# Attention with FFN beside it: query scratch stored once and split on load, head stores ahead of loads, first head's rows loaded earlier

## What is computed

```python
xn = _layernorm(x)
q = _rope(split(xn @ Wq + bq)); k = _rope(split(xn @ Wk + bk)); v = split(xn @ Wv + bv)
scores = jnp.einsum('bhnd,bhmd->bhnm', q, k) / jnp.sqrt(256)
inter = jnp.einsum('bhnm,bhmd->bhnd', softmax(scores), v)
attn = inter @ Wo + bo
# FFN with weights +1/-1 from booleans; h starts as [xn, -xn]
h = relu(s0 * (h @ w0)) * 2; h = relu(s1 * (h @ w1)) * 2; h = s2 * (h @ w2)
return x + attn + h
```

## Time and profile before

| | |
|---|---|
| median of 3 runs (lowest, highest) | 2648.79 us (2647.93, 2649.21) |
| profiled execution, its own time | 2645.93 us |
| its span, first to last instruction | 2644.1 us |
| busy: TensorE, ScalarE, VectorE, GpSimd | 2577.4, 2099.3, 977.5, 300.0 us |
| preparation (to 240.48 us), attention (from there) | 240.48, 2403.62 us |

### The profile page before, as it was taken

The page is one execution under the profiler, slowest core; times in us unless marked ns, Lnnn a source line. Parts: engine busy times, 40 slices in busy tenths (PEclk is TensorE's granted clock), DMA queues, the critical chain, the costliest instruction groups (busy, mean ns, idle before and its releaser), DMA issues.

```text
span 2644.1 us, 49178 instructions
## 1 busy us (share of the span) xinstructions
PE 2577.4 (97%) x20711; PEld 1340.4 (51%) x20711; DVE 977.5 (37%) x1665; ACT 2099.3 (79%) x2342; POOL 300.0 (11%) x268
## 2 busy tenths in 40 slices
PE   7886999999999999999999999999999999999999
PEld 5663454444445454545445454544445454544545
DVE  7773323343324233243324233243324233242323
ACT  6885888888888878788887878788887878788884
POOL 6783000000000000000000000000000000000000
PEclk9997999999999999999999999999999999999999
DMA  9995111111212112121212212121212212121212
GB/s 283 294 292 171 37 47 52 53 61 49 57 43 75 51 48 71 50 77 53 78 44 70 63 46 70 53 77 51 77 43 67 61 53 69 57 77 49 77 38 97
DMA packets 202199, 210.45 MB, mean 80 GB/s; under 512 B 144685, under 2 KB 148605, under 8 KB 195577
## 3 DMA queue, kind: packets, MB, share of 16 engines
q1 hardware_dynamic: 199672, 198.91, 25.1%
q10 hardware_dynamic: 2304, 8.39, 0.9%
HBM read 131.34 MB, written 75.89 MB: 78 GB/s over the span
## 4 chain that ended last, share of the span: by engine, by line
PE 91%; ACT 0%; DVE 0%; issue 0%; DVEq 0%; SPq 0%
PE ps_o L1042 37%; PE ps_f L1075 27%; PE ps_s L1029 24%; PE ps_y L1088 2%; PE ps_s L1124 0%; PE ps_f L1124 0%; ACT probs L1009 0%; DVE probs L1266 0%; PE ps_f L1132 0%; PE ps_o L1124 0%; PE ps_y L1124 0%; PE ps_s L1132 0%; DVEq L819 0%; PE ps_o L1132 0%; PE ps_y L1132 0%
## 5 line engine op out<-in xcount | busy, mean ns | idle before, releaser
L1009 ACT ACTIVATE probs<-ps_s 128x1024 f32<-128x1024 f32 x2048 | 1930.0, 1034 | 453.1 <-PE ps_s L1029 450.7
L1042 PE MATMUL ps_o<-probs,v_ones 128*32 128x512 f32 x8192 | 1011.3, 600 | 0.0
L1029 PE MATMUL ps_s<-q_rows,k_rows 50*128 50x512 f32 x4096 | 868.9, 439 | 5.1 <-SPq L981 4.1
L1029 PEld LDWEIGHTS ps_s<-q_rows,k_rows 50*128 50x128 f32 x4096 | 365.7, 184 | 672.2 <-ACT probs L1009 600.3
L1042 PEld LDWEIGHTS ps_o<-probs,v_ones 128*32 128x32 f32 x8192 | 200.6, 108 | 418.3 <-issue 295.8
L1075 PE MATMUL ps_f<-h_hi,ffn_w 64*128 64x512 f32 x2048 | 410.2, 393 | 0.0
L1075 PE MATMUL ps_f<-h_lo,ffn_w 64*128 64x512 f32 x2048 | 409.3, 391 | 0.0
L1209 DVE COPY raw<-ps_f 128x512 f32<-128x512 f32 x256 | 164.9, 686 | 560.4 <-PE ps_f L1075 560.4
L1164 POOL TENSOR_TENSOR heads<-heads,sums 128x512 f32<-128x512 f32 x64 | 82.3, 1285 | 2149.8 <-DVE sums L1185 2149.8
L1185 DVE RECIPROCAL sums<-sums 128x128 f32<-128x128 f32 x256 | 226.6, 924 | 1.7
L1075 PEld LDWEIGHTS ps_f<-h_lo,ffn_w 64*128 64x128 f32 x2048 | 198.7, 186 | 34.2
(11 more groups left out here) (118 smaller groups left out, 1384.6 us busy)
## 6 DMA issues: line engine op xcount, KB each, us to landing
k_rows<-k_parts SPq DMA_DIRECT2D x128, 256.0 KB
q_rows<-q_parts SPq DMA_DIRECT2D x384, 64.0 KB
q_parts<-parts SPq DMA_DIRECT2D x32, 512.0 KB, 8.7
k_parts<-parts SPq DMA_DIRECT2D x32, 512.0 KB, 8.3
k_rows<-k_parts SPq DMA_DIRECT2D x128, 128.0 KB
x_chunk<-in_x ACTq DMA_DIRECT2D x16, 512.0 KB, 7.3
xn_d<-xn_t SPq DMA_DIRECT2D x16, 512.0 KB, 8.6
v_heads<-v_sb SPq DMA_DIRECT2D x16, 512.0 KB, 7.7
```

What stands on the lines that cost most here:

```text
L1009: nc.scalar.activation(probs[:, s % PBUF, half * 2 * C:(half + 1) * 2 * C], ps_s[:, half].rearrange("p c n -> p (c n)"), ACT.Exp, scale=SC ...
L1029: last = nc.tensor.matmul(ps_s[:, half, w], k_rows[rows, u, t * P:(t + 1) * P], q_rows[rows, u, half], start=True, stop=True)
L1042: last = nc.tensor.matmul(ps_o[32 * c:32 * c + 2 * DH], v_ones[:, u, t], probs[:, s % PBUF, c * C:(c + 1) * C], start=(t == 0), stop=(t == ...
```

## The change

**Queries.** The scratch for q holds the full fp32 value once (2 tiles per chunk of 128x512) instead of a high and a low part. GpSimd writes q's `turned` tile straight into `parts` (two buffers per j, by `c % 2`), ScalarE only squares it, SP stores it. For k nothing changes but the indices. On load, the three row groups of a head all read the same q rows. VectorE then rounds the whole tile into `q_hi` and subtracts `q_hi` times a mask that is 1 on the low rows only: the low rows become the low part, the others keep the full value, which the matmul reads as fp32r. This runs in the seventh round (n % 10 == 6) of the head before. The loads of a head are split into queries, shift and keys, in that order, with a semaphore of their own for queries and shift.

**First head.** Its queries are loaded at chunk 7, xT_lo at 8, its keys at 9 and 11 (halves). GpSimd splits the queries at the end of chunk 8 (three operations). The rows' zeroing moves from DMAs to a GpSimd memset. `store_shift` of the bound moves from SP's to ScalarE's queue. `bv` and `bo` are loaded at chunk 4 instead of 5. One small table `lo_rows` (128x1) is loaded ahead of Wv.

**Heads.** `heads` and `sums` have one buffer instead of two. `store_head` is ahead of `load_head`. `finish` waits for all earlier heads' stores and for GpSimd's product of the last head.

```diff
-FIRST_HEAD_AT = 13
+FIRST_QUERIES_AT = 7
+SPLIT_QUERIES_AT = 6
...
+                if c == FIRST_QUERIES_AT:
+                    sp.wait_ge(k_rows_set, 1)
+                    load_queries(sp, scratch, 0, w["q_rows"][:, 0], first_q_loaded)
+                if c == FIRST_QUERIES_AT + 1:
+                    sp.dma_start(w["xT_lo"][:].bitcast(F32).rearrange("p k n -> p (k n)"), scratch["xn"][0]).then_inc(first_x_loaded, 16)
+                if c in (FIRST_QUERIES_AT + 2, FIRST_QUERIES_AT + 4):
+                    load_keys(sp, scratch, 0, w["k_rows"][:, 0], first_loaded, [(c - FIRST_QUERIES_AT) // 2 - 1])
...
             def part(n):
-                c, j, u = n // 4, n % 4, n % PART_BUFS
+                c, j = n // 4, n % 4
...
-                nc.scalar.activation(square[:, c % 2, j], turned[:, n % 3], ACT.Square).then_inc(square_ready, 1)
-                if n >= PART_BUFS:
-                    act.wait_ge(parts_stored[u], 16 * (n // PART_BUFS))
-                nc.scalar.activation(parts[:, u, 0], turned[:, n % 3], ACT.Copy).then_inc(part_high, 1)
+                if j < 2:
+                    nc.scalar.activation(square[:, c % 2, j], parts[:, j, c % 2].bitcast(F32), ACT.Square).then_inc(square_ready, 1)
+                    return
+                k_out_of = turned[:, (2 * c + j - 2) % 3]
+                nc.scalar.activation(square[:, c % 2, j], k_out_of, ACT.Square).then_inc(square_ready, 1)
+                if c > 0:
+                    act.wait_ge(parts_stored[j], 16 * c)
+                nc.scalar.activation(parts[:, j, 0], k_out_of, ACT.Copy).then_inc(part_high, 1)
...
+                if c == FIRST_QUERIES_AT + 1:
+                    pool.wait_ge(first_q_loaded, 16 * 6)
+                    nc.gpsimd.tensor_copy(w["q_hi"][:].bitcast(F32R), first_q.bitcast(F32)).then_inc(first_q_high, 1)
...
+                    nc.gpsimd.tensor_tensor(w["q_hi"][:], w["q_hi"][:], w["lo_rows"][:, 0:1].broadcast_to([P, 2 * C]), ALU.mult).then_inc(first_q_high, 1)
...
+                    nc.gpsimd.tensor_tensor(first_q, first_q.bitcast(F32), w["q_hi"][:], ALU.subtract)
...
             def load_head(g, u):
-                load_rows(sp, scratch, g, q_rows[:, u], k_rows[:, u], rows_loaded[u])
+                load_queries(sp, scratch, g, q_rows[:, u], q_loaded[u])
+                load_shift(sp, scratch, g, q_rows[:, u], q_loaded[u])
+                load_keys(sp, scratch, g, k_rows[:, u], rows_loaded[u])
...
+                    if HEADS * i + j > 0:
+                        pe.wait_ge(q_split, HEADS * i + j)
...
             def finish(i, j):
-                u = j % 2
-                dve.wait_ge(heads_stored[u], 32 * CB * i + 16 * CB * (j // 2 + 1))
+                for u in range(2):
+                    dve.wait_ge(heads_stored[u], 16 * CB * ((HEADS * i + j + 1 - u) // 2 + 1))
+                    dve.sem_inc(tail_begun, 1)
+                if HEADS * i + j > 0:
+                    dve.wait_ge(heads_ready, HEADS * i + j)
+                    dve.sem_inc(tail_begun, 1)
...
+            def split_queries(g):
+                u = g % 2
+                at = q_rows[:, u].rearrange("p h n -> p (h n)")
+                dve.wait_ge(q_loaded[u], 16 * QUERY_LOADS * ((g + 1) // 2))
+                nc.vector.tensor_copy(q_hi[:].bitcast(F32R), at.bitcast(F32)).then_inc(q_step, 1)
+                dve.wait_ge(q_step, g)
+                dve.sem_inc(tail_begun, 1)
+                nc.vector.scalar_tensor_tensor(out=at, in0=q_hi[:], scalar=w["minus_lo"][:, 0:1], in1=at.bitcast(F32),
+                                               op0=ALU.mult, op1=ALU.add).then_inc(q_split, 1)
```

More of the change, by code:

```diff
@@ L266, in prepare, with store_shift @@
         block = ctx.enter_context(nc.Block())
+        def store_shift(queue, a, filled, landed):
+            to = scratch["shift"][a].rearrange("g (h w n) -> w (g h) n", h=P // G, n=FILL)
+            for n in range(G * N // (P * FILL)):
+                queue.dma_start(to[n], filled.bitcast(F32)).then_inc(landed, 16)
         def here(c):
@@ L272, in _ @@
         def _(sp):
-            def store_shift(a, filled, landed):
-                to = scratch["shift"][a].rearrange("g (h w n) -> w (g h) n", h=P // G, n=FILL)
-                for n in range(G * N // (P * FILL)):
-                    sp.dma_start(to[n], filled.bitcast(F32)).then_inc(landed, 16)
             sp.dma_start(ident[:], a["ident"]).then_inc(ident_loaded, 16)
@@ L292, in _ @@
             sp.wait_ge(zero_ready, 1)
[L293 removed]
+            store_shift(sp, 1, fill[:], fill_stored)
             def store_x(c):
@@ L851, in attend @@
         rows_loaded = [sem(f"rows_loaded{u}") for u in range(2)]
+        q_loaded = [sem(f"q_loaded{u}") for u in range(2)]
         v_loaded = [sem(f"v_loaded{u}") for u in range(2)]
@@ L953, in one_pass @@
                     u = j % 2
+                    if j == HEADS - 1 and last:
+                        begin_last()
+                    if j >= 1:
+                        store_head(i, j - 1)
                     if not last or j < 2:
```

187 lines of the change are left out of this document (110 added, 77 removed).

## The result

The changed kernel takes 2623.72 us (median; 2623.01 to 2623.82, four runs), the kernel before on the same chip 2648.36 us (2647.56 to 2649.21, four runs). The ratio is 0.9906, 95% interval 0.9889 to 0.9923: 24.6 us or 0.9% faster. The profiled execution took 2623.64 us with a span of 2621.9 us, against 2645.93 and 2644.1 before.

The account below looks back on a forecast made before the run. It took TensorE to bound attention, and bytes, closely followed by ScalarE and TensorE, the preparation's chunks. -13.4 - 2.5 - 11 + 6 + 3 = -17.9 from 2645.93 gave 2628.0, plus 2.86 for the median: 2631 us, range 2614 to 2643.

Parts of the forecast that it names:

- Ten chunks: Preparation from 63.83 us: smaller query stores and two fewer ScalarE copies bring chunks from 12.64 to 11.3 us, 13.4 us gained.
- The moved loads: First head's loads, now in chunks 7 to 11, delay key stores: about 2 us for each of three batches, 6 us lost.
- GpSimd's split: First head's queries: three GpSimd operations, at most 8.0 us, with 3.3 us free per chunk; 3 us lost.
- Last three chunks: End of the preparation, without the loads at chunks 13 and 14: 27.9 us instead of 38.93, 11 us gained, ends 8 to 15.
- Chunks 0 to 2: Start of the preparation: 1.6 MB fewer bytes, 5 us, of which half was taken: 2.5 us gained.
- Tail: Serial stretch between last chunks and attention: `store_shift` on ScalarE's queue changes 0, ends -1.9 and +1.
- attention: Attention stage: VectorE's added split, 121 us of work in 63 heads, fits into slack; 0, ends 0 and +3.
- B: Rival, 12%: bytes decide throughout and the moved loads fit into slack; 8.4 MB less at 291 GB/s is 28.8 us, 2620.
- A: Rival, 20%: ScalarE's work, not the bytes, bounds the chunks; 16.6 us gained less 9 for moved work, about 2641.
- C: Rival, 8%: the first head's work at chunks 7 to 11 eats the gain; no gain, about 2648.
- D: Rival, 5%: in attention the split comes too late for TensorE; slower, from 2660 to 2752.
- what was to show the steps right: Signs: ten chunks in about 113 us, last three in 28, no ScalarE query-store waits, key-store wait, GpSimd block 5 to 8, attention undisturbed.

Follow-up runs that it names:

- e_factors: The changed kernel with VectorE's `factors` of a chunk moved behind the fourth pair of products: 2618.0 us, ratio 0.9887.
- e_spread: The changed kernel with GpSimd's three operations on the first head's queries spread over the ends of chunks 8, 9 and 10: 2620.96 us, ratio 0.9901.
- e_before_early: The kernel before with only the first head's loads moved, from chunks 13 and 14 to 7 and 8: 2646.18 us, ratio 0.9995.
- e_bytes: The changed kernel with each query store issued twice, the second to a scratch that nothing reads (8.4 MB back): 2642.64 us, ratio 0.9982.
- e_split3: The changed kernel with VectorE's rounding of a head's queries to their high part made three times instead of once, in 63 heads: 2622.29 us, ratio 0.9907.
- e_shift_sp: The changed kernel with the first head's row of bounds stored by SyncE, as in the kernel before, instead of ScalarE: 2623.93 us, ratio 0.9912.
- e_act: The changed kernel with two ScalarE copies per chunk added in place of those removed, result unused: 2630.64 us, ratio 0.9937.

## Why the prediction came out as it did

The forecast was 2631.0 us in a range of 2614 to 2643; measured were 2623.72 and a gain of 24.6 where the sum had 17.9. Step by step:

- **Ten chunks, pace 11.3 us (-13.4).** The size was right, the reason was not: that is luck. Ten chunks of 11.37 us would be 113.7, 12.7 less than before; the stalls (1.7 and 0.5 at the loads, 3.9 for GpSimd's block with the short chunk behind it) make up the rest of the 119.77. But I took 11.3 as a mixture of bytes (10.8), ScalarE (10.5) and TensorE (10.1), three busy sums. What sets it is a circle through three engines with no single one full: VectorE is busy for 101.94 of 119.77 us, ScalarE for 97.66, GpSimd for 81.72. Cutting it (e_factors) gave chunks of 10 to 11 us. Before, ScalarE's work did fill such a chunk, and I subtracted two copies from it without following what the chunk would wait for next. Half of that could be read before: VectorE waited for ScalarE there, and `shift_ln` took up to 0.96 us in other chunks.
- **The moved loads (+6).** Three stalls of 2 us were expected. The first measured 1.7 us (13.04 - 11.37), the last 0.5 (11.88), and the one between them is hidden in GpSimd's block; in e_spread, where it isn't, the three make 4.4 us. So three stalls came as expected, somewhat smaller: the term was too dear by 4 us as the kernel stands and by 1.6 without the block. The working behind it is not sound. The 7.2 us were those of a half and of xT_lo, 1088 KB, and I scaled them as if they were the half's 576 alone; 384 of 1088 KB give 2.5 us, which the 3 us of slack would have covered. And the slack is larger, for a key store lands in 4.8 us now (median) and not in the 8.3 that I left standing: 6.5 us instead of 3. That stalls are left all the same shows that landing behind such a batch takes more than either sum had: the store that ScalarE waits for until 116.91 was issued from 107.14 on. By the rule of the Trainium skill that I weighed ("DMA: Bandwidth & Descriptors", section on why a DMA increments its semaphore by 16), these stalls would have been nearer 12 us; the waits are against it. No row shows single DMA engines, so only its price falls here, not the rule.
- **GpSimd's split (+3).** Its chunk grew by 5.2 us, its full 5.3, and the next one gave 1.3 back: 3.9 us, near the forecast. The 3.3 us of free time were not free where the block stands, for GpSimd stands in the circle. e_spread got 2.3 us of the pair back (1.6 over the ten chunks), and what stays there is the stall of the key loads.
- **Last three chunks (-11).** They gave 16.27, the largest error. I priced them as 11.2 + 11.2 + 5.5; they took 10.02, 9.16 and 3.48. My 11.2 was the pace of the chunks ahead, but no FFN weights are converted here and the statistics have ended, so ScalarE and VectorE have less to do, and TensorE alone sets the pace of the first two: it is busy for all of their 10.02 and 9.16 us at clock 1.00 (windows, as above):

```profile
184.15:194.17 10.02, 10.02 (x62) 8.34 (x61) 7.60 (x11) 7.70 (x13) 7.66 (x6) 1.00 0.91 294
194.17:203.33 9.16, 9.16 (x54) 7.52 (x53) 6.04 (x10) 4.33 (x8) 7.64 (x6) 1.00 0.85 258
```

Before, these two took 17.24 and 15.68 us at 0.84 and 0.83, and the drain 6.01 at 0.50. e_before_early shows that the loads' going is worth 11.8 us by itself, near the 11 of the prediction, and the clock comes back with it: 10.12 and 9.98 us at 1.00. The rest is mostly the drain's, and there it is the smaller stores: 3.48 us after, 6.55 with the bytes put back (e_bytes), while the two chunks ahead of it keep their 10.04 and 9.15. How much of the 11.8 is the clock's no run separates. The upper end of 15 was the better number.
- **Chunks 0 to 2 (-2.5).** They lost 0.55. The DMA share fell from 0.90 to 0.80 and the length stayed, and e_bytes with its bytes back has 64.32, so transfers did not set it. e_factors, which shortens them by 3.9 us (64.38 to 60.50), shows that VectorE's order had a part in it.
- **Tail (0), attention (0).** From the last `ps_n` matmul to the first scores the tail lost 0.91 us, inside its ends, and attention took 1.08 more, inside its ends and inside the scatter of that stage. e_split3 shows that the split isn't the reason; e_shift_sp leaves 0.7 of the tail's 0.9 to ScalarE's queue, below what the runs can tell.
- **The rivals.** B (bytes decide throughout, 2620) was nearer to the measured time than the forecast. By e_bytes its first half is right, three quarters of the gain hang on bytes. Its rate is not: 8.4 MB at 291 GB/s are 28.8 us, and 18.9 came back. A falls with e_act, and the 358 GB/s that I weighed for it is passed here (one slice of 5.5 us of the kernel after moved 390); C falls with the waits (9.8 us where it had 15.5 for the loads alone), D with e_split3. Of what was to show the steps right, the end of ScalarE's query waits, the key-store wait behind the query load (2.47 us), the block of 5.3 us and the undisturbed attention came; the last three chunks took 22.66 us, not 28; and "ten chunks in about 113 us" was said without the 9 us that the prediction itself added for them: with these it is 122, against 119.77.

What stays open: why `e_factors` differs from after by 5.7 us in the medians and by 2.0 in the profiled pair (its runs reach from 2617.65 to 2621.68, and the profiled one is the slowest), how much of the last three chunks' gain is the clock's, what the loads' move is worth with the smaller stores, and what GpSimd's missing low parts are worth.

## What to carry to other kernels

Read a loop's period from chunks that have no stall, and follow it around all engines before subtracting an operation from it. Here the same length, 11.37 us, had one cause before and another after; 19 us of ScalarE's work put back cost some 7 us, 8.4 MB of stores put back some 19. A load that is moved takes its stall along: in the kernel before, the move was worth nothing. Put a large one-off job on an engine in the circle in pieces, one per round; here that was worth 1.6 to 2.8 us, little more than the runs can tell.

## What the runs showed of the hardware

A VectorE operation on 128x4 elements takes 0.16 us or up to 1.27. In the kernel before `shift_ln` takes 0.16 to 0.96 us (median 0.20), after 0.16 to 1.27 (median 1.24). Of its 32 executions in the two kernels, the 7 with no GpSimd operation beside them take 0.16 us. Each of the other 25 begins while a GpSimd operation runs and ends with it: never ahead of its end, at most 0.10 us behind. After, the 12 long ones (1.22 us or more) begin 0.04 to 0.09 us behind a join's start, as 100.77 to 102.02 beside 100.70 to 101.99 above. Before, the 5 of 0.93 to 0.96 us stand beside the subtraction for the low part:

```profile
120.19 0.95 DVE L596 SCALAR_TENSOR_TENSOR shift_ln<-moments,rstd 128x4 f32<-128x4 f32 x1
```

```profile
119.84 1.28 POOL L550 TENSOR_TENSOR parts<-turned,parts 128x512 fp32r<-128x512 f32 x1
```

VectorE's products, which read one operand from PSUM, don't show this: L639 takes 0.74 us at 101.94, with GpSimd idle, and 0.74 at 103.85, beside a join. The same as for `shift_ln` is seen in attention, where GpSimd's product of a head falls beside the split in some heads, first after, then in e_split3:

```profile
275.37 2.06 DVE L1265 SCALAR_TENSOR_TENSOR q_rows<-q_hi,minus_lo,q_rows 128x1024 fp32r<-128x1024 f32 x1 [0.16 <-DVE q_hi L1262]
```

```profile
275.01 1.65 DVE L1264 CAST q_hi<-q_rows 128x1024 fp32r<-128x1024 f32 x1
276.70 0.69 DVE L1266 CAST q_hi<-q_rows 128x1024 fp32r<-128x1024 f32 x1
277.55 1.28 DVE L1269 SCALAR_TENSOR_TENSOR q_rows<-q_hi,minus_lo,q_rows 128x1024 fp32r<-128x1024 f32 x1 [0.16 <-DVE q_hi L1266]
```

In e_split3 the two added copies stand where the subtraction stood; now the first of them is the long one (1.65 against 0.69 us), and the subtraction has its 1.28 us back. So it is what stands beside it in time that makes the operation long, not its shape. GpSimd's product is longer as well in such heads, 1.60 us instead of 1.29. I had not expected it: the prediction priced the split at 1.92 us, and where it falls beside the product it takes 0.63 + 2.06.

The Trainium skill says why such a thing can be: "SBUF — State Buffer", section "Who interferes with whom", has VectorE and GpSimd share one pair of ports, held by one of them for a whole instruction, and names VectorE operations with two inputs in SBUF against a GpSimd operation that reads SBUF. The rows of `shift_ln` and of the subtraction, both with two inputs in SBUF, agree with it. The long copy in e_split3 has one input; the section names casts as well, for a mode with two ports, and no row here shows in which mode it ran. No run separated the ports from other causes.
